# A retimed opening: weight loads issued from ScalarE and new stage tables in a four-layer sequence kernel

## The reference, cut to what matters

```python
# layers 0 and 3 (linear attention with FiLM)
xn = layernorm(x); q, k, v = xn @ Wq + bq, xn @ Wk + bk, xn @ Wv + bv   # k and v masked
q = softmax(q by head over features); k = softmax(k over tokens)
y = q @ (k^T @ v) by head
h = layernorm(y) * (1 + scale) + shift          # scale, shift = silu(cond) @ W_emb + b
x = x + silu(h) @ W_out + b_out

# layers 1 and 2 (Mamba; layer 2 on permuted tokens)
shift, scale, gate = split(silu(cond) @ W_ada + b_ada, 3)
h = layernorm(x) * (1 + scale) + shift
u, z = split(h @ W_in); u = silu(conv4(u)); dt_r, B, C = split(u @ W_x)
dt = softplus(dt_r @ W_dt + b_dt); A = -exp(A_log)
state = state * exp(dt * A) + dt * u * B        # 512 steps, for 512 channels x 16 states
y = (sum over states of state * C) + u * D_param
x = x + gate * ((y * silu(z)) @ W_out)
```

## Time and profile before

| | |
|---|---|
| median of 3 runs | 2298.06 us (2295.0 to 2298.16) |
| profiled execution, its own time | 2298.16 us |
| its span, first to last instruction | 2296.3 us |
| mean granted TensorE clock | 0.925 |
| busy: PE, DVE, ACT, POOL | 84%, 87%, 76%, 84% |
| first scan starts | 125.19 us |

### The profile page before, as it was taken

The page is one execution under the profiler, slowest core; times in us unless marked ns, Lnnn a source line. Parts: engine busy times, 40 slices in busy tenths (PEclk is TensorE's granted clock), DMA queues, the critical chain, the costliest instruction groups (busy, mean ns, idle before and its releaser), DMA issues. The chain is left out here.

```text
span 2296.3 us, 23859 instructions
## 1 busy us (share of the span) xinstructions
PE 1928.1 (84%) x5712; PEld 989.9 (43%) x5712; DVE 1995.3 (87%) x2730; ACT 1756.3 (76%) x2739; POOL 1920.3 (84%) x1610
## 2 busy tenths in 40 slices
PE   6867788898988989898888888889899978777886
PEld 5432334345453544435454443435445443323353
DVE  4379998989999899999989999998989989898962
ACT  3578778787988779798787969788897978778643
POOL 0179999979898998989898998988898898999950
PEclk9879899999999899999999999999998989889997
DMA  6155665655556565655555565555456555565620
GB/s 232 33 142 156 177 177 152 177 146 164 147 169 166 157 181 156 181 159 156 149 149 168 161 194 156 160 168 159 145 161 174 158 165 174 165 177 167 188 67 19
DMA packets 170555, 358.84 MB, mean 156 GB/s; under 512 B 19545, under 2 KB 27953, under 8 KB 161713
## 3 DMA queue, kind: packets, MB, share of 16 engines
q1 hardware_dynamic: 151958, 279.32, 37.3%
q0 software_dynamic: 9216, 67.11, 15.4%
q10 hardware_dynamic: 9242, 10.89, 1.4%
HBM read 284.85 MB, written 5.29 MB: 126 GB/s over the span
## 5 line engine op out<-in xcount | busy, mean ns | idle before, releaser
L664 POOL TENSOR_TENSOR state<-state,c_rows 128x512 f32<-128x512 f32 x1024 | 1315.3, 1351 | 129.9 <-DVE state L1139 64.8
L1445 PE MATMUL bank<-state,const_sb 128*128 128x512 f32 x1536 | 769.5, 619 | 70.5 <-POOL state L664 65.2
L1142 DVE TENSOR_TENSOR_SCAN state<-decay,bank 128x512 f32<-128x512 f32 x640 | 764.1, 1206 | 29.9 <-ACT decay L891 28.4
L883 ACT ACTIVATE bank<-b_rows 128x512 f32<-128x512 f32 x640 | 379.8, 593 | 251.2 <-DVE state L1139 162.7
L655 POOL TENSOR_TENSOR state<-kept,b_rows 128x512 f32<-128x512 f32 x384 | 512.3, 1334 | 0.1
L1132 DVE TENSOR_TENSOR bank<-kept,bank 128x512 f32<-128x512 f32 x640 | 436.1, 681 | 83.9 <-ACT bank L883 81.6
L1139 DVE TENSOR_TENSOR_SCAN state<-bank,state 128x512 f32<-128x512 f32 x384 | 466.5, 1215 | 3.6 <-POOL state L655 3.2
L891 ACT ACTIVATE decay<-kept,ssm_pack 128x512 f32<-128x512 f32 x640 | 454.7, 710 | 2.4 <-ACT x_dbl L830 1.2
L1445 PEld LDWEIGHTS bank<-state,const_sb 128*128 128x128 f32 x1536 | 287.2, 197 | 388.0 <-issue 212.5
L875 ACT ACTIVATE bank<-kept,ssm_pack 128x512 f32<-128x512 f32 x384 | 260.7, 679 | 73.2 <-DVE state L1142 62.0
L1343 PE MATMUL bank<-kept,ssm_pack 128*128 128x512 f32 x512 | 252.5, 626 | 38.2 <-DVE kept L1092 18.6
(11 more groups left out here) (136 smaller groups left out, 2009.8 us busy)
## 6 DMA issues: line engine op xcount, KB each, us to landing
b_rows<-flat_rows SPq DMA_DIRECT2D x512, 256.0 KB, 3.4
c_rows<-flat_rows SPq DMA_DIRECT2D x512, 256.0 KB, 3.3
state<-state POOLq DMA_DIRECT2D x64, 1024.0 KB, 8.3
out<-x_res ACTq DMA_DIRECT2D x8, 512.0 KB, 3.0
ssm_pack<-ssm_pack SPq DMA_DIRECT2D x2, 2035.0 KB, 12.1
x_next<-x ACTq DMA_DIRECT2D x6, 512.0 KB, 4.5
state<-ada_w SPq DMA_DIRECT2D x1, 1536.0 KB, 11.7
kept<-ada_w SPq DMA_DIRECT2D x1, 1536.0 KB, 14.0
```

The lines of the kernel that those rows point to most:

```text
L664: pool.tensor_tensor(st, st, c_rows[:, row % ROWS], ALU.mult).then_inc(m_prod, 1)
L883: act.activation(mix_banks[g % BANKS][:], b_rows[:, row % ROWS], ACT.Copy).then_inc(m_brow, 1)
L1142: ins = dve.tensor_tensor_scan(st, decay[:, nth(g) % DECAYS], mixed, 0.0, ALU.mult, ALU.add)
L1445: pe.matmul(y_banks[c2][:], ident, state[:, g % STATES], start=False, stop=(g == in_bank[-1])).then_inc(m_sum, 1)
```

## The change

Five loads leave SP's list and are issued by ScalarE behind its silu of `cond`: the two gate rows, ada_w 1, ada_w 2 and ssm_pack 2. The unit ranges of setup, prep 0 and attention 1 are new, and so are the stage tables of attention kinds "first" (attention 0), "second" (attention 1) and "last" (attention 15), of prep "first", of post 3, of tail 0 and of the setup.

```diff
-SETUP_UNITS, FIRST_PREP, FIRST_ATT = (-137, -68), (-76, -10), (-66, 28)
+SETUP_UNITS, FIRST_PREP, FIRST_ATT = (-139, -68), (-81, -18), (-70, 34)
...
-    "first": (29, 11, 41, 7, 34, 41, 66, 5, 44, 46, 1, 0, 36, 10, 16, 39, 19, 3, 30, 0, 62, 36, 12, 64, 27, 11, 27,
-              16, 33, 1, 36, 57, 11, 54, 41, 0, 51, 114, 47, 29, 42, 2, 38, 19, 40, 6, 66, 1, 17, 0, 40, 9),
-    "second": (13, 0, 3, 5, 5, 13, 9, 5, 4, 20, 9, 0, 3, 20, 7, 3, 17, 11, 3, 15, 9, 29, 0, 4, 0, 4, 3, 1, 0, 3, 20,
-               10, 5, 16, 4, 7, 5, 5, 7, 3, 9, 8, 12, 0, 10, 0, 5, 6, 0, 10, 20, 0),
+    "first": (24, 15, 12, 14, 10, 33, 0, 28, 37, 17, 0, 19, 32, 25, 0, 0, 7, 5, 46, 22, 55, 40, 2, 6, 21, 32, 27, 32,
+              23, 2, 30, 34, 27, 45, 40, 14, 64, 56, 69, 9, 13, 26, 31, 4, 0, 15, 65, 3, 3, 4, 36, 1),
+    "second": (1, 1, 0, 0, 1, 3, 6, 4, 1, 2, 4, 6, 3, 11, 0, 6, 6, 0, 4, 5, 5, 2, 9, 27, 5, 4, 6, 2, 1, 2, 0, 3, 1, 2,
+               1, 5, 0, 1, 1, 1, 5, 2, 1, 0, 0, 0, 3, 8, 2, 9, 0, 0),
...
-    "first": (2, 0, 10, 13, 28, 35, 7, 4, 23, 9, 0, 12, 8, 8, 15, 26, 5, 11, 37, 1, 12, 20, 4, 1),
+    "first": (4, 3, 0, 23, 6, 11, 19, 7, 0, 4, 15, 5, 2, 23, 2, 12, 6, 15, 6, 0, 5, 6, 20, 3),
...
-    3: (0, 10, 11, 4, 1, 11, 4, 34, 18),
+    3: (7, 0, 2, 21, 2, 14, 30, 31, 5),
...
-    0: (7, 107, 23),
+    0: (18, 81, 25),
...
-SETUP_STAGES = dict(zip(SETUP_NAMES, (58, 6, 9, 37, 34, 91, 27, 57, 3, 20, 10, 42), strict=True))
+SETUP_STAGES = dict(zip(SETUP_NAMES, (42, 6, 13, 9, 12, 65, 19, 20, 0, 20, 11, 44), strict=True))
...
-            sp.dma_start(ada_sb[1], ada_w[1].rearrange("(k p) n -> p k n", p=P)).then_inc(s_cond_w[1], 16)
...
-            sp.dma_start(ada_sb[2], ada_w[2].rearrange("(k p) n -> p k n", p=P)).then_inc(s_cond_w[2], 16)
...
-            for n in range(2):
-                sp.dma_start(gate_bias[:, n], gate_rows[n].partition_broadcast(B)).then_inc(s_gate_rows, 16)
-            sp.dma_start(ssm_sb[2][:], ssm_packs[2]).then_inc(s_ssm_w[2], 16)
...
+            for n in range(2):
+                act.dma_start(gate_bias[:, n], gate_rows[n].partition_broadcast(B)).then_inc(s_gate_rows, 16)
+            for layer in SSM:
+                act.dma_start(ada_sb[layer], ada_w[layer].rearrange("(k p) n -> p k n", p=P)).then_inc(s_cond_w[layer], 16)
+            act.dma_start(ssm_sb[2][:], ssm_packs[2]).then_inc(s_ssm_w[2], 16)
```

More of the change, by code:

```diff
@@ L95 @@
           0, 1, 3, 0, 7, 2, 1, 0, 1, 7, 4, 0, 4, 0, 2, 0),
-    "last": (1, 20, 3, 11, 15, 0, 2, 38, 15, 56, 30, 19, 96, 32, 65, 130, 1, 12, 17, 66, 46, 26, 34, 14, 1, 11, 60,
-             12, 8, 4, 39, 12, 21, 7, 6, 10, 35, 54, 60, 0, 0, 9, 89, 0, 32, 23, 19, 11, 37, 46, 56, 9),
+    "last": (27, 7, 5, 13, 41, 23, 19, 35, 0, 85, 3, 17, 83, 0, 14, 101, 1, 37, 10, 31, 66, 20, 0, 9, 40, 18, 43, 12,
+             2, 13, 29, 2, 50, 8, 3, 10, 12, 21, 82, 12, 10, 22, 78, 0, 41, 4, 10, 28, 35, 6, 0, 7),
 })
 PREP_STAGES = by_name(PREP_NAMES, {
-    "first": (2, 0, 10, 13, 28, 35, 7, 4, 23, 9, 0, 12, 8, 8, 15, 26, 5, 11, 37, 1, 12, 20, 4, 1),
+    "first": (4, 3, 0, 23, 6, 11, 19, 7, 0, 4, 15, 5, 2, 23, 2, 12, 6, 15, 6, 0, 5, 6, 20, 3),
     0: (1, 2, 5, 6, 5, 4, 2, 1, 3, 0, 7, 6, 3, 5, 1, 0, 2, 2, 2, 7, 2, 12, 3, 2),
```

## The result

The changed kernel takes 2321.53 us (median of 10 runs, 2315.31 to 2328.55), the kernel before 2305.41 us in the same comparison (10 runs, 2295.0 to 2316.62): ratio 1.0066, 95% interval 1.0038 to 1.0095. It is slower, by about 15 us, where I forecast 2297.3 and no difference. (Ratios are estimated over all runs of both kernels; they are not quotients of the medians.) The median of before is higher here than the 2298.06 shown above, since five of these ten runs took 2310.2 to 2316.6; over the 35 runs beside each later set about a third lie as high, and the median is 2298.2 to 2299.1. The profiles of experiments 1, 8 and 9 are of such executions: TensorE stays at 1.2 GHz through most of the first attention. That this is so in every run of the upper group is inferred from the times.

What follows compares the result with a forecast made beforehand. Bound by a 125 us opening, 1024 scan units keeping GpSimd fed, and a serial end. Terms -2.0 + 1.4 + 0.5 + 0.0 - 0.7 = -0.8 us from 2298.16 gave 2297.4, stated as 2297.3; range 2290.5 to 2304.5.

Steps and rivals of the forecast that it cites:

- Part 3: Opening loads: five DMA issues moved from SP to ScalarE lose 0 to 5.8 us, taken as 0.5, mask row's lateness included.
- rival (b): Opening: ScalarE is held in its DMA issues as SP was, giving 2302.6 us; chance 0.09.
- Part 1: Way to the first scan: attention 1's later stages move behind it, so the scans start 2.0 us earlier.
- it comes out even: Work reordered from 78 to 106 us: kexp0 earlier by 1.3, silu of u2/u3 ending about 98.1 instead of 97.9.
- Part 2: First attention: c1 after v1 and kT0 makes matt 1.0 us late, k1.0 behind k0 another 0.4; loss 1.4.
- Part 4: Scans 0 to 64: denser prep 1 loses 1.0 us, spreading attention 1 offsets it; 0 net.
- Rival (c): Scans 0 to 64: prep 1 too dense, extra waits of 4 to 6 us, 2301 to 2303.5; chance 0.12.
- My bound of 4: Prep 1 in 26 units: loss at most 4 us, most of the 5.5 GpSimd idles in that stretch, once more.
- Part 5: Later scans and end: post 3's changes cost 0 in the scans, the end is 0.7 us shorter.
- hidden by GpSimd, 0: Post 3 in scans 4, 8, 12: gw earlier and add later cost nothing, each site within 1 us.
- Rival (a): Scans 0 to 64: order better for GpSimd, removing 5 of 7.2 us idle, 2292.3; chance 0.19.
- (d): TensorE's clock, 42 to 78 us: a shifted clock change moves the time by +-2 us, counted within the same case.

Runs made afterwards that it cites:

- experiment 1: Kernel before with only the five loads moved from SP to ScalarE, all tables old: 2313.86 us against 2298.22, ratio 1.0031.
- experiment 8: Kernel before with only ssm_pack 2 moved to ScalarE, behind the silu: 2302.45 us against 2298.52, ratio 1.0008.
- experiment 9: Kernel before with attention 1 from kT0 on at the new units (end at 34, prep 1 in 26): 2304.51 us against 2299.1, ratio 1.0019.
- experiment 2: Changed kernel with the five loads back on SP, so only the tables are new: 2310.92 us against 2298.22, ratio 1.0024.
- experiment 10: Kernel before with new setup and first-attention tables, attention 1 late from kT0 (end at 31), prep 1 at 31 to 63: 2295.81 us against 2299.1.
- experiment 5: Kernel before with only the new tables of setup and first attention, and the setup's units: 2301.41 us against 2298.52, ratio 0.9988.
- gw alone: Kernel before with only VectorE's gw in post 3 moved ahead of one injection and one subtraction: 2312.96 us against 2299.1, ratio 1.0034.

## Why the prediction was wrong

**Part 3, the loads: this step failed, and it is the largest.** The prediction says of the mask row: "how long it takes, the trace does not show, and I count its lateness in the same 0.5". It measured 9.7: 6.95 by the store and 3.91 by the load back, less 1.16 to spare. I had bounded the cost of the *issues* on ScalarE from both sides, and that part held in its result: the five stood from 5.22 (during the table load of the silu, so earlier than I had them) to 9.01 us, 1.99 of it in the last, and `xn` at 9.05 lay inside the free time up to 10.4, so rival (b) did not happen. The store and load of the mask row had no bound and no rival of its own. Yet before showed the store's 4.0 us, on which SP's next issue hangs, and film_w in flight to 12.4. The rival that I left out is that a chain store, completion, load, k0 is stretched by whatever else is in flight.

The Trainium skill (DMA: Bandwidth & Descriptors, Issuing engines are not separate DMA queues) says that transfers from all issuers run on the same 16 DMA engines and interleave. The traces agree, and show how: by packets about evenly (62 and 52 in experiment 8), and so by time not at all (98.6 and 1.5%). I had used the rule only for bandwidth, "the move gains nothing"; it also spoke against the change.

**Part 1, start of the scans: the gain was there, a loss ahead of it was not seen.** dt to the first scan is 2.1 shorter (forecast 2.0), with the first decay 2.6 nearer to dt, as forecast. VectorE's 16.0 us wait for the product ahead of `matt` is now one of 14.27 for ScalarE. The step that failed is "it comes out even" for what is reordered between 78 and 106 us: x0 to dt is 2.9 longer (4.4 in experiment 2), since kexp1 comes late and TensorE's next products fall to 1.2 GHz. Experiments 9 and 10, with the old order there, have 33.1 and 31.9.

**Part 2 was right in its number and half right in its terms:** +1.4 forecast, +1.4 measured (1.7 in experiment 5). m1 starts 24.3 us behind k0 instead of 23.3, the 1.0 of the forecast, and in experiment 2 `matt` starts directly behind the permutation. The other 0.4 was luck: k1's first two products behind k0 run at 2.4 GHz (1.12 us), not at the slow clock, but `mix` falls to 1.2 GHz (2.75 us instead of 2.02; the granted clock of 49.2 to 52.6 us is 0.50), and `matt` waits 0.36 for it.

**Part 4, scans 0 to 64:** the mechanism was right, the sizes were not. I took +1.0 for prep 1 in 26 units and -1 for the spread of attention 1; measured were +7.4 and -3.5, in sum 4.0 instead of 0. Rival (c), 4 to 6 us with a chance of 0.12, comes nearest, by its clause on more waits; but the waits lie in units 32 to 50, and scan unit 64 waits for nothing (units 50 to 64 take 27.9 against 27.8). My bound of 4 came from GpSimd's idle time in the old stage; two waits of over 4 us each went beyond it.

**Part 5, post 3 and the end:** "hidden by GpSimd, 0" was wrong. All five kernels with the new post 3 take 1963.8 to 1967.5 us from unit 64 to the last scan, the eight others with the old 1955.7 to 1959.3, and gw alone 1960.4. So it costs some 5 to 10 us. Of it gw ahead of the subtraction is 1.8 by its waits (0.6 in each of three scans); its kernel is 3.3 longer in this stretch, of which the rest is the clock and within the spread of single profiles. How the rest divides between `add` and the output products stays open. The 0.7 at the end is not shown: the end takes 86.6 instead of 89.0, but six kernels with the old tables there have 87.1 to 87.6.

**The sum:** forecast -2.0 + 1.4 + 0.5 + 0 - 0.7; measured (9.7) + (1.4) + (2.9 - 2.1) + 1.5 (matt to x0: experiments 2 and 5, with the same order there, have it 0.8 shorter instead; the granted clock of that stretch is 0.68 against 0.75) + 4.0 + 6.7 - 2.3 = 21.8, the 21.9 of the spans but for rounding. Rival (a) did not happen, and (d) is in the 1.5.

## What to carry over

When a load is moved to another engine, ask first what small transfer is on a chain while the load is now in flight, and price that chain (store, completion, load back, first use), not only the issues. Price it by packets: the small transfer's packets for each engine, times what one packet of the other queue takes, until one of the two has run out. An order tuned by hand has few free places: work moved out from ahead of the first scan had to be paid for where it landed, and a range of units taken from one chain of work cost more than the other won, unless both ends were moved. And price an instruction of an in-order engine by what it covered in its old place: gw filled a wait for TensorE, and ahead of it it left the wait open.

## What was unexpected in the hardware

A store of 48 KB in 784 packets took 4.0 us beside one load, 8.0 beside 1.5 MB more, 9.3 beside 2.0 MB more in 16 KB packets and 11.1 beside 5.1 MB more. Two queues took turns by packets, not by bytes: 399 packets of 64 bytes beside 400 of 3 KB in 3 us.

The same program had TensorE at 2.4 GHz from 19.1 us on in one execution and from about 57 us in another (17.6 us between them). In the second the profile's granted clock reads 1.00 from 15 to 60 us, while a 128x256 group of four takes 2.08 us. The trace's first record of the clock is at 58.0 us there (19.0 in before), and the view prints 1.00 for the time ahead of it: up to the first record the length of the matmuls tells the clock and the column does not. That holds for k0 in the earlier trace rows too. Kernels with the new tables of the setup and the first attention seem not to have this, by their times alone: their five sets of 12 runs spread by 4.2 to 11.6 us and the changed kernel's ten by 13.2, while the seven sets of 12 with the old ones spread by 18.8 to 27.7. Which piece of the new order does it was not tried.
